# Plain fp32 scores in the second attention, GpSimd's share of the first chunk's drive, and eight expert pairs ahead of the second scan

## What is computed

```python
xn = layernorm(x)
x = x + attention(xn) + experts14(xn)     # 8 heads, causal; top 1 of 14 experts, 128 -> 256 -> 128, gelu
xn = layernorm(x)
x = x + scan(xn) + experts8(xn)           # state scan; top 2 of 8 experts, 128 -> 512 -> 128, relu
# attention: q, k = x@W + b + sinusoid; softmax(q k^T / sqrt(128)) v; out @ Wo
# scan: u, res = x@W_in; u = silu(u); delta = softplus(u@W_delta + b); B, C = u@W_B, u@W_C
#   h = exp(delta*A)*h + delta*B*u;  y = sum over 16 states of h*C;  out = (y + u*D)*silu(res) @ W_out
```

## Time and profile before

| what | us |
|---|---|
| median of 3 runs | 923.66 (919.79 to 923.72) |
| the profiled execution | 924.14, span 922.3, PE clock 0.88 |
| busy: PE, DVE, ACT, POOL | 717.9 (78%), 558.4 (61%), 415.5 (45%), 250.2 (27%) |
| the scatters by POOL (L500), x48 | 1.136 each |
| load of a 256 KB expert matrix by SP, to landing | 4.5 |

### The profile page before, as it was taken

The page is one execution under the profiler, slowest core; times in us unless marked ns, Lnnn a source line. Parts: engine busy times, 40 slices in busy tenths (PEclk is TensorE's granted clock), DMA queues, the critical chain, the costliest instruction groups (busy, mean ns, idle before and its releaser), DMA issues. The chain is left out here.

```text
span 922.3 us, 11738 instructions
## 1 busy us (share of the span) xinstructions
PE 717.9 (78%) x3526; PEld 512.6 (56%) x3527; DVE 558.4 (61%) x848; ACT 415.5 (45%) x828; POOL 250.2 (27%) x199
## 2 busy tenths in 40 slices
PE   4889999999899176786888878785747877786665
PEld 2656666666578142564655555563246776675223
DVE  5264333334223114978888988958708767557688
ACT  1254555555434146546655564542714444544220
POOL 0012112111000301522324133320160354344882
PEclk9999999999979667989997999876967898988778
DMA  9200000000459101235457446653533343431111
GB/s 314 58 3 10 10 9 11 9 6 4 144 152 333 47 1 60 63 100 114 129 139 178 103 120 168 144 140 107 104 116 97 107 129 113 131 108 46 37 40 55
DMA packets 59797, 86.65 MB, mean 94 GB/s; under 512 B 7505, under 2 KB 35922, under 8 KB 59762
## 3 DMA queue, kind: packets, MB, share of 16 engines
q1 hardware_dynamic: 41330, 57.89, 20.1%
q0 software_dynamic: 7680, 23.08, 11.6%
q10 hardware_dynamic: 10752, 5.24, 1.9%
HBM read 54.60 MB, written 14.81 MB: 75 GB/s over the span
## 5 line engine op out<-in xcount | busy, mean ns | idle before, releaser
L983 PE MATMUL PS<-ROOM 128*128 128x512 f32 (+3 forms) x384 | 162.1, 537 | 3.5 <-ACT ROOM L660 3.5
L1472 DVE TENSOR_REDUCE nmax<-PS 128x1 f32<-128x128 f32 (+7 forms) x128 | 96.1, 751 | 76.1 <-PE PS L955 72.4
L660 ACT COPY ROOM<-PS 128x512 f32<-128x512 f32 (+1 forms) x192 | 86.1, 482 | 121.9 <-PE PS L967 121.5
L514 POOL TENSOR_TENSOR QL<-ROOM,QH 128x512 fp32r<-128x512 f32 x32 | 44.0, 1375 | 319.0 <-ACT QH L652 319.0
L942 PE MATMUL PS<-KH,QH 128*128 128x512 f32 (+1 forms) x192 | 90.7, 472 | 49.1 <-POOL QL L514 47.9
L667 ACT ACTIVATE ROOM<-PS,nmax 128x128 f32<-128x128 f32 (+7 forms) x128 | 96.1, 751 | 51.9 <-DVE nmax L1472 51.9
L967 PE MATMUL PS<-CST,ROOM 128*128 128x128 f32 x576 | 91.9, 290 | 18.1 <-ACT ROOM L667 16.9
L967 PEld LDWEIGHTS PS<-CST,ROOM 128*128 128x128 f32 x576 | 72.0, 149 | 57.7 <-issue 38.9
L983 PEld LDWEIGHTS PS<-ROOM 128*128 128x128 f32 x384 | 70.8, 211 | 34.4 <-issue 27.6
L1546 DVE TENSOR_TENSOR_SCAN ROOM<-ROOM 128x1024 f32<-128x1024 f32 x32 | 79.3, 2477 | 3.4 <-ACT ROOM L698 3.2
L942 PEld LDWEIGHTS PS<-KH,QH 128*128 128x128 f32 x192 | 40.0, 208 | 69.3 <-POOL QL L514 33.8
(11 more groups left out here) (173 smaller groups left out, 1252.8 us busy)
## 6 DMA issues: line engine op xcount, KB each, us to landing
ROOM<-bc_rows SPq DMA_DIRECT2D x32, 512.0 KB, 5.0
ROOM<-ROOM POOLq DMA_DIRECT2D x32, 512.0 KB, 5.7
ROOM<-in_w SPq DMA_DIRECT2D x56, 256.0 KB, 4.5
ROOM<-in_w SPq DMA_DIRECT2D x32, 321.0 KB, 4.0
rows_in<-zero SPq DMA_DIRECT2D x20, 256.0 KB, 3.4
ROOM<-rows_in SPq DMA_DIRECT2D x24, 128.0 KB
rows_out<-ROOM ACTq DMA_DIRECT2D x24, 128.0 KB, 1.8
ROOM<-rows_in SPq DMA_DIRECT2D x8, 256.0 KB, 4.0
```

What stands on the lines that cost most here:

```text
L660: nc.scalar.copy(dst, src).then_inc(s_ed, 1)
L983: r = mm(PS[:, 6, lo:BANK], V[:, j, :], PT[:, 4 * group + j, lo:BANK], start=j == 0, stop=True, skip_group_check=True)
L1472: nc.vector.tensor_reduce(nmax[:, i % 4:i % 4 + 1], sc[:, 0:(i + 1) * P], AX_X, ALU.max, negate=True).then_inc(s_nm, 1)
```

## The change

Batch 1's attention makes its scores by one plain fp32 product of K1 and Q1, which DVE writes directly; ACT's and POOL's part in the query goes. POOL makes the drive of half c = 0 of each state of batch 0 (`low_drive`), DVE that of c = 1 (`high_drive`). K1, Q1 and 2 x 1024 further numbers a partition lie where the four halves lay (`LATER`), and hold the pairs' first matrices, rows and hidden layers afterwards, so that pairs 0 and 1 are loaded when the last scores are done. `AHEAD` is 8 and `LATE` 8: eight pairs run before state 0, late states are 8 to 15 with four gathers each. The order of the change-over is new on PE, ACT and DVE; state 14 moves ahead of `head_end(15)`. In `two_pairs` the expert numbers are loaded behind the hidden products and the next pair is turned ahead of `between`. ACT reads `pair_in` before `pair_out`. Left out of the diff: bank numbers, names of semaphores, and the ScalarE guards on the query.

```diff
-AHEAD = 4
+AHEAD = 8
 LATE = (2 * PAIRS - AHEAD) // 2
...
+with ExitStack() as first_split:
+    KH, KL, QH, QL = (first_split.enter_context(nc.sbuf_tensor(n, [P, T], F32R)) for n in ("KH", "KL", "QH", "QL"))
+LATER = sb("LATER", [P, 4 * T])
+K1, Q1 = LATER[:, 0:T], LATER[:, T:2 * T]
...
-mw1 = room(HEAD_END, [4, 4 * P])
-at = HEAD_END + 8 * KB
-MX1 = room(at, [4, D])
-MXT1 = room(at + 2 * KB, [2, P])
-MY1 = room(at + 3 * KB, [4, D])
-c_half = room(at + 5 * KB, [BANK])
-MH1 = HS0.rearrange("p (i n) -> p i n", n=P)
+mw1 = LATER[:, 2 * T:4 * T].rearrange("p (i n) -> p i n", i=4)
+MH1 = K1.rearrange("p (i n) -> p i n", n=P)
+MX1 = Q1[:, 0:BANK].rearrange("p (i n) -> p i n", n=D)
+c_half = Q1[:, BANK:T]
+MXT1 = room(48 * KB, [2, P])
+MY1 = room(49 * KB, [4, D])
...
-        sp.wait_ge(s_xhc, 2 * STATE)
+        def second_matrices(experts):
+            for e in experts:
+                sp.dma_start(second_w[:, e, :], A["w_1"][e][:, 4 * P:8 * P]).then_inc(s_mw2, 16)
         sp.wait_ge(s_eid, 2)
         sp.wait_ge(s_sc[1], 16 * TB * MOE[1][1])
+        sp.wait_ge(s_ex, 16 * TB)
         rows(0, 0)
         rows(1, 1)
+        second_matrices((7, 0, 1, 2))
+        sp.wait_ge(s_pv, 4 * HEADS)
+        second_matrices((5, 6))
+        sp.wait_ge(s_wo, 4 * HEADS)
+        second_matrices((3, 4))
         with sp.Fori(1, PAIRS // 2) as r:
...
+    def low_drive(n):
+        pool.wait_ge(s_xbl[n % 2], 16 * (n // 2 + 1))
+        if n:
+            pool.wait_ge(s_xsn, 2 * n - 1)
+        else:
+            pool.wait_ge(s_du, 1)
+        nc.gpsimd.tensor_tensor(DB, DU0[:, 0, :], BS[:, n % 2, :], ALU.mult).then_inc(s_xdp, 1)
...
     def attention_second():
-        query_low(HEADS, 0)
         for t in range(TB, NT):
-            if t == TB + 3:
-                query_low(HEADS, 1)
             gather(0, 0, t, GA[:, t, :], s_g0[1])
-        query_low(HEADS + 1, 0)
+        low_drive(0)
         for h in range(1, HEADS):
             n = 2 * h - 2
+            low_drive(n + 1)
             y_add(n, 0)
-            query_low(HEADS + h, 1)
+            y_add(n, 1)
             if h == 1:
                 pool.wait_ge(s_slot, 2)
             scatter(1, range(TB * (h - 1) // (HEADS - 1), TB * h // (HEADS - 1)))
-            y_add(n, 1)
-            if h < HEADS - 1:
-                query_low(HEADS + h + 1, 0)
+            low_drive(n + 2)
             y_add(n + 1, 0)
             y_add(n + 1, 1)
-        for n in (STATE - 2, STATE - 1):
-            y_add(n, 0)
-            y_add(n, 1)
+        y_add(STATE - 2, 0)
+        low_drive(STATE - 1)
+        y_add(STATE - 2, 1)
+        y_add(STATE - 1, 0)
+        y_add(STATE - 1, 1)
...
     def attention_second():
-        query_high(8, 0)
-        head(8, False, True, after={7: (0, 0)})
+        head(8, False, True, split=False, after={7: (0, 0)})
...
-            head(g, True, g < 15, after={0: (n, 1), 2: (n + 1, 0), 3: (n + 1, 1), 6: (n + 2, 0)})
+            head(g, True, g < 15, split=False, after={0: (n, 1), 2: (n + 1, 0), 4: (n + 1, 1), 6: (n + 2, 0)})
...
         act.wait_ge(s_da1, 5 * b + 4)
+        if b:
+            act.wait_ge(s_r3, 1)
         nc.scalar.activation(S2b[b], S1b[b], ACT.Exp, scale=-1.0).then_inc(s_da1, 1)
...
-    deviation(3)
-    take_transposed(3)
-    inner(1)
     first_decay(STATE - 1, 0)
     first_decay(STATE - 1, 1)
-    skip(1)
-    step_sizes(1)
-    act.wait_ge(s_xhc, 2 * STATE)
     pair_in(0)
+    deviation(3)
     pair_hidden(0)
     pair_in(1)
+    take_transposed(3)
     pair_out(1, 0, None)
     pair_hidden(1)
-    gate_exp(2)
-    logarithm(1)
+    inner(1)
+    pair_in(2)
     pair_out(2, 1, None)
-    pair_in(2)
     pair_hidden(2)
+    step_sizes(1)
     pair_in(3)
     pair_out(3, 0, 16)
     pair_hidden(3)
+    gate_exp(2)
+    logarithm(1)
+    skip(1)
+    for p in range(4, AHEAD):
+        pair_in(p)
+        pair_out(p, (p - 1) % 2, 16 * ((p - 1) // 2))
+        pair_hidden(p)
     def beside(n, p, times):
+        pair_in(p)
         pair_out(p, 1, times)
-        pair_in(p)
         pair_hidden(p)
         pair_in(p + 1)
         pair_out(p + 1, 0, times + 16)
...
-            three(PS[:, s + lo // BANK, 0:hi - lo], (QH, QL), (KH, KL), q, (slice(None), slice(lo, hi)), True)
+            dst = PS[:, s + lo // BANK, 0:hi - lo]
+            if b:
+                mm(dst, Q1[:, i * P:(i + 1) * P], K1[:, lo:hi], start=True, stop=False, skip_group_check=True)
+            else:
+                three(dst, (QH, QL), (KH, KL), q, (slice(None), slice(lo, hi)), True)
...
     def head(g, b, h, s, pending, follow):
-        pe.wait_ge(s_qe, 2 * g + 1)
+        s_query = s_qr if b else s_qe
+        pe.wait_ge(s_query, 2 * g + 1)
...
     def result_pair(p, es):
-        if not (isinstance(p, int) and p == 0):
+        if isinstance(p, int) and p == 0:
+            pe.wait_ge(s_we, 4 * HEADS)
+            pe.wait_ge(s_mw2, 16 * MOE[1][0])
+        else:
...
+            if b and q >= 2:
+                pe.wait_ge(s_dr, 4 * b + q - 1)
+            elif b and q == 1:
+                pe.wait_ge(s_lgr, 3)
...
-    def two_pairs(p, times, between=None):
-        first, second = experts_of(p), experts_of(p + 1)
-        turn_pair(p, 0, times)
+    def two_pairs(p, times, between, more=True):
         hidden_pair(p, 0, times)
+        es = ids(p)
         turn_pair(p + 1, 1, times)
-        result_pair(p, first)
+        result_pair(p, es)
         hidden_pair(p + 1, 1, times)
-        if between:
-            between()
-        result_pair(p + 1, second)
+        es = ids(p + 1)
+        if more:
+            turn_pair(p + 2, 0, times + 1)
+        between()
+        result_pair(p + 1, es)
+    pe.wait_ge(s_eid, 2)
+    turn_pair(0, 0, 1)
+    hidden_pair(0, 0, 1)
+    es = ids(0)
+    turn_pair(1, 1, 1)
     transposes(3)
+    result_pair(0, es)
+    hidden_pair(1, 1, 1)
+    es = ids(1)
     logits(3)
     inner(1)
+    turn_pair(2, 0, 2)
+    result_pair(1, es)
+    hidden_pair(2, 0, 2)
+    es = ids(2)
+    bc_rows(1)
     step_sizes(1)
+    turn_pair(3, 1, 2)
+    result_pair(2, es)
+    hidden_pair(3, 1, 2)
+    es = ids(3)
     ranks(2)
-    bc_rows(1)
-    pe.wait_ge(s_dr, 8)
+    for p in range(4, AHEAD):
+        turn_pair(p, p % 2, p // 2 + 1)
+        result_pair(p - 1, es)
+        hidden_pair(p, p % 2, p // 2 + 1)
+        es = ids(p)
+        if p == 5:
+            scan_out(0)
     pe.wait_ge(s_rkr, 3)
-    pe.wait_ge(s_lgr, 3)
-    pe.wait_ge(s_eid, 2)
-    pe.wait_ge(s_mw2, 16 * MOE[1][0])
-    two_pairs(0, 1)
-    two_pairs(2, 2)
-    scan_out(0)
-    pe.wait_ge(s_r3, 1)
     pe.wait_ge(s_as, 2)
     spread_b(0, False)
+    turn_pair(AHEAD, 0, AHEAD // 2 + 1)
+    result_pair(AHEAD - 1, es)
     pe.wait_ge(s_oe, 2)
     pe.wait_ge(s_eid, 3)
     for n in range(SHARED + 1):
         spread_c(n, n > 0, False)
         two_pairs(AHEAD + 2 * n, AHEAD // 2 + n + 1, lambda: spread_b(n + 1))
-    with pe.Fori(SHARED + 1, LATE) as n:
+    with pe.Fori(SHARED + 1, LATE - 1) as n:
         spread_c(n)
         two_pairs(AHEAD + 2 * n, n + AHEAD // 2 + 1, lambda: spread_b(n + 1))
+    spread_c(LATE - 1)
+    two_pairs(2 * PAIRS - 2, PAIRS, lambda: spread_b(LATE), False)
     spread_c(LATE)
...
+            if b:
+                dve.wait_ge(s_kf, q + 3)
+                ts(K1[:, sl], QF, SCALE, None, ALU.mult).then_inc(s_ke, 1)
+                continue
...
     def q_evac(g, hf, first=False):
         dve.wait_ge(s_qp, 2 * g + hf + 1)
-        if not first:
+        if not first and batch[0] == 0:
             dve.wait_ge(s_qe, 2 * g + hf)
         h = g - 8 * batch[0]
-        stt(QF, bank(7), bq[:, bass.ds(h, 1)], peT[:, hf * BANK:(hf + 1) * BANK], ALU.add,
+        to = Q1[:, hf * BANK:(hf + 1) * BANK] if batch[0] else QF
+        stt(to, bank(7), bq[:, bass.ds(h, 1)], peT[:, hf * BANK:(hf + 1) * BANK], ALU.add,
             ALU.add).then_inc(s_qr, 1)
...
     def first_state(n):
-        first_drive(n, 0)
-        first_drive(n, 1)
-        for c in range(2):
-            first_scan(n, c)
-            first_c(n, c)
+        first_scan(n, 0)
+        first_c(n, 0)
+        high_drive(n)
+        first_scan(n, 1)
...
             head(g, True, g < 15, g > 9, after={
-                0: (lambda: first_drive(n, 0), lambda: first_drive(n, 1)),
-                1: (lambda: first_scan(n, 0), lambda: first_c(n, 0)),
+                0: (lambda: first_scan(n, 0),),
+                1: (lambda: first_c(n, 0), lambda: high_drive(n)),
                 2: (lambda: first_scan(n, 1),),
-                3: (lambda: first_c(n, 1), lambda: first_drive(n + 1, 0)),
-                4: (lambda: first_drive(n + 1, 1),),
-                5: (lambda: first_scan(n + 1, 0),),
-                6: (lambda: first_c(n + 1, 0),),
-                7: (lambda: first_scan(n + 1, 1), lambda: first_c(n + 1, 1))})
+                3: (lambda: first_c(n, 1),),
+                4: (lambda: first_scan(n + 1, 0),),
```

(11 more changed lines are left out.)

57 lines of the change are left out of this document (28 added, 29 removed).

## The result

The changed kernel takes 867.61 us (median of 4 runs, 865.15 to 872.14) where the kernel before takes 922.01 (4 runs, 919.79 to 923.72): a ratio of 0.9417, 95% interval 0.937 to 0.9464. That is 54.4 us less; 42 were forecast. The profiled execution took 868.27 us, span 866.3. A later repeat of both kernels gave 857.54 against 906.54 us, 0.946 (0.9381 to 0.9538).

A forecast was written before the change was run, and what follows sets the result against it. No engine bounds the whole: second-attention heads wait on the query chain, the change-over on engine-to-engine handoffs, paired states on TensorE, late states on VectorE. Attention -20, change-over +2, second scan -24: -42 from 924.14 gives 882 us, range 860 to 903.

The forecast's parts named there:

- rival B: Second attention: with the query chain gone TensorE stays at full clock, heads 27 to 28 us, 864 us; chance 0.11.
- Second scan, -24 forecast: Paired states 92.2 plus late states 77 us, 169 against 193.6 us; bounds -37 and -8.
- I take 12.0 us for a looped state: Second scan: a looped state with two pairs falls from 13.7 to 12.0 us; bounds 10.9 and 13.7.
- Attention, -20 forecast: Second attention: seven heads 2.2 us shorter each, -15.4, and head 8 starting about 4.6 us earlier.
- +1.25 us of TensorE a head: Second attention: plain fp32 scores cost TensorE 1.25 us more a head, 26.9 to 28.2 us.
- the release is a state ahead, so I cost the order at nothing: Second attention: the drive's place in GpSimd's queue behind two scatters and four additions into y costs 0 us.
- rival A: Second attention: each GpSimd drive locks out a two-input VectorE instruction, 2 x 2.1 us a head; 897 us; chance 0.14.
- Change-over, +2 forecast: Last head's addition to second scan: -12 stand, -8 and -2 filled or moved, +20 four pairs, +4 new wait; bounds -12, +14.
- -12 for the stand: Change-over: TensorE's stand of about 12 us, beside GpSimd's sixteen scatters, goes.
- rival C: Change-over: the stand beside the scatters comes back on pair 4 or 5, +12, 894 us; chance 0.14.
- Rival D: Change-over: a 12.1 us stand for every pair beside the scatters; two give 906 us, four 930; chance 0.08.
- rival E: Second scan and attention: loop keeps 13.7 us a state and heads 32 us, 905 us; chance 0.05.

The follow-up runs named there:

- first traces: The first profiled executions of the kernel before and the changed kernel, no further edit; medians 922.01 and 867.61 us, ratio 0.9417.
- the one chip: Later repeat of the kernel before and the changed kernel on one chip, no edit; 906.54 and 857.54 us, ratio 0.946.
- second trace of the changed kernel: Profile of the changed kernel from the later repeat, no edit against the changed kernel; median 857.54 us, ratio 0.946.
- the count with four ahead: Changed kernel with four pairs ahead of the second scan instead of eight (AHEAD = 4); 852.27 us, ratio 0.9418.
- the kernel with the reads in front: Changed kernel with both expert-number reads (four register loads) put back to the front of the two pairs; 865.02 us, ratio 0.9558.

## Why the prediction was right, and where it was not

The direction and the range were right (867.6 us in 860 to 903, 882 forecast). That the sum came near is in part luck: the second scan gave 16 to 19 us more than forecast, the attention and the change-over together 8 to 15 less, and the two errors partly cancel. The 867.6 us also lie near rival B's 864, but not for rival B's reason. One of the three changes, the move of the drives, was a loss, which the forecast did not have.

**Second scan, -24 forecast, -40.5 measured (204.4 to 163.9), -43.3 in the first traces.** The mechanism was named, the term "I take 12.0 us for a looped state" was mis-sized. Its floor of 10.9 us, the written-out state of before, was no floor: the written-out state had its own gap of 1.41 us and that went too. A looped state takes 9.9 us. Paired states: 78.4 us where the forecast had 92.2. The late ones: seven of eight take 8.35 us, VectorE's own time, and one 13.9; 72.4 us against 77 forecast. Four gathers a state do keep up. The range to 10.9 was my bound from the nearest row, which was itself a row with the fault in it. The reads behind the products, named in the forecast, are what did it; the turning ahead, named beside them, gives nothing by itself.

**Attention, -20 forecast.** The wait at the start of head 8 came out: the scores follow VectorE's sum by 1.18 us instead of 6.10, 4.9 us earlier against 4.6. (In the traces head 8's first maximum comes 2.0 us earlier on the one chip and 8.0 in the first traces, since the stretch of experts before it differs by some us from trace to trace.) Head 8 itself is 1.4 us longer (28.0 against 26.6), which had no term. Heads 9 to 14 give 1.5 us each and not 2.2; from the start of head 9 to the last addition the stretch falls by 237.6 - 231.7 = 5.9 us, with one more state of the first scan in it, which the forecast had booked in the change-over. The two steps that failed are opposite. What goes with the plain scores was priced too small: alone they take 3.6 us off a head, and the clock goes from 0.91 to 0.99 with it. Of rival B (TensorE at full clock, heads at 27 to 28 us) that is the half that is true. The +1.25 us of TensorE a head does not show in its busy time, which went from 26.9 to 26.2 us where the forecast had 28.2; no run here tells the price of the scores from the clock. And "the release is a state ahead, so I cost the order at nothing" was wrong: the second drive of a head stands behind the scatters and starts beside the product with C. The forecast had named that meeting as probable and gave the meetings 1.4 us a head; it is 2.2 us of VectorE a head (13.1 us in six products), at a place where TensorE's next maximum waits, and the whole move costs 1.9 us a head instead of giving. That is rival A at half its size: one drive of two meets an instruction at full price, the other falls beside instructions that read PSUM, as the forecast had it for the first.

The Trainium skill, SBUF — State Buffer, section "SBUF: two separate sides", says that the pair of ports is locked for a whole instruction and the loser stands until it is free. The trace agrees in size: a product of 1.2 us that comes 0.08 us behind a drive of 2.38 takes 3.39 us, and 1.2 + 2.38 - 0.08 is 3.5.

**Change-over, +2 forecast, +6.4 measured, +2.3 in the first traces.** The walk was right in its order: a stand of 10.7 us before pair 4 that ends with ScalarE's copy behind the logarithm, then pairs in series. The two pairs did not fill the wait for the normalisation: only the first one's hidden products lie in it, 4.55 us of the 8.5 are left, and the rest of both pairs comes behind the transposes. A pair in series takes 3.8 us in the second trace of the changed kernel and 3.4 in the count with four ahead; 4.7 was taken. The term that failed is "-12 for the stand": the stand beside the scatters that it was to remove is not in every run of the kernel. It is missing in the kernel before when that is run again, and came back in the first trace of the changed one, on pair 6, which was rival C. Without it the forecast's terms give +14; four pairs at 13.5 instead of 20 bring that to 7.5, near the 6.4 measured. So here too two errors partly cancelled. With the forecast's own state moved to the attention, attention and change-over together were to give 18 us; they gave 4.9 - 1.4 + 5.9 - 6.4 = 3.0 on the one chip and 4.9 - 1.4 + 8.4 - 2.3 = 9.6 in the first traces.

**Rival D** (a stand for each pair beside the scatters) and **rival E** (loop and heads unchanged) fell: pairs 5 to 7 ran without a stand in the changed kernel's second trace, the loop is at 9.9 us.

The measured signs in "what the new profile would show" were right but for three: the looped states lie below the 11 to 13 us named; one late state of eight takes 13.9 us; and "few scans over 3 us" was true while the products, which I had not named there, took the slowing.

## What to carry to other kernels

Before a short instruction is moved to an idle engine that can hold up the busy one, look at what stands ahead of it in its new queue and what the busy engine does when it starts: the same drive cost 1.9 us a head behind two scatters and gave 1.2 ahead of them. Register reads in TensorE's own stream belong under products that are already queued; four in front of a looped state left a gap of 2.25 to 2.5 us, and the lower clock that followed it in some states cost up to 1.6 us more. When work is moved from one stage to another, price it anew at the speed the source stage will have after the rest of the change, since the gain of moving pairs was gone once a paired state took 9.9 us.

## What was not expected of the hardware

The granted clock of the second attention moved with small changes of order that left TensorE's work as it was: 0.93 in the changed kernel's heads 9 to 14, 0.98 with the drive ahead of the scatters, 0.99 with the plain scores alone, 0.95 with the drive on VectorE. A head of 28 to 29 us goes with the high values, and which is cause and which effect was not tried.

A gap of some 2.3 us in TensorE's work was not always followed by a lower clock. In the kernel with the reads in front, the sixteen products behind a gap of 2.26 us took 2.05 us (granted clock 1.00), behind one of 2.25 in the next state 2.83 (0.69); behind 2.53 us plus two transposes and 0.54 us they took 3.63 to 3.68 in every looped state (0.54 in the one shown).

What the "remote" stand of the first two traces is stays open. In it several engines stood for 8 to 11 us although the records of the products that they waited for had ended. It was in both kernels there and in no later trace, with the same scatters in the same place. The medians of the kernel before, 922 and 904 to 909 us, differ by about its length, which speaks for it being in the unprofiled runs of the first measurement too; this was not shown.
